# Flamingo-style block on one core: where the attention denominators are inverted and spread, and where the dispatch buffer is zeroed

## The chip, the core and the metric

One core of one Trainium2 chip. Its engines are TensorE (PE; PEld is its weight load), VectorE (DVE), ScalarE (ACT), GpSimd (POOL) and SyncE (SP), which here only issues DMAs; GpSimd issues DMAs too. The metric is device time in microseconds, and lower is better. Each engine works through its own list in order, and waits are semaphore waits, so what stands behind a waiting instruction on its engine waits too.

## The reference

```python
x = x + tanh(g_xattn[0]) * L0_xattn(layernorm(x), ctx)      # 16 heads of 16, softmax over 512 keys
x = x + tanh(g_ffn[0])   * L0_ffn(layernorm(x))             # mixture of 8 experts, top 2, capacity 1280
x = x + tanh(g_xattn[1]) * L1_xattn(layernorm(x), ctx)      # the same attention, other weights
x = x + tanh(g_ffn[1])   * L1_ffn(layernorm(x))             # fp8-quantised linear layer

p = softmax(q k^T / 4);  out = p v;  merged @ wo
buf = zeros(E*C + 1, D).at[pos].set(xk)                     # the dispatch buffer, E*C = 10240 rows of 1 KB
```

x is (8, 512, 256) in float32: 8 batches of 512 tokens, 256 wide. The softmax of both attentions is what the change touches: its exponentials are multiplied with the values first, and the division by their sum comes after.

## The kernel before

The kernel is ten stages, each a block in which all engines start together and which ends when all are done: setup, project, attention (layer 0), route, place, experts, combine, attention (layer 1), merge, quantise.

**Attention** walks through 32 groups (8 batches of 4 groups, each of 4 heads). Per group TensorE forms scores twice. First come eight units for the maxima (`max_unit`, L795), which VectorE reduces (`reduce`, L884) and turns (`turn_maxima`); SyncE then moves the negated maxima nT into four spare rows of q with four DMAs (`subtract_maxima`, L714, tile a_nT). Then come eight score units (`score_unit`, L805), from whose product the maximum is already subtracted; the first unit of a group waits for those four DMAs. ScalarE exponentiates (L867), and TensorE multiplies with v (`values`, L819), whose 17th column of ones gives the sum of the exponentials, the denominator. ScalarE takes the result to osb (L859). SyncE stores it to memory (`outs`, L718) and loads it back as 64 rows of BIG (L722) and as denominators (d_den, L723). GpSimd meanwhile issues the loads of the group four ahead (`load_group`, ten DMAs, L683 to L695), and once a batch the load of v (L765).

**Division** (`class Division`) inverts a batch's denominators on VectorE (`invert`, L612), stores them to `dens` (`store`, L617, four DMAs), loads them back so that each head's row of 1024 reciprocals stands in its 16 partitions (`broadcast`, L626, two DMAs with a source repeated 16 times, into wide), and multiplies BIG by wide on GpSimd (`scale`, L632). Batches 0 to 5 pass through this inside the attention block, 8 to 10 groups late; batches 6 and 7 (`EARLY = 6`) at the start of the next block. SyncE's program in the attention block sets the order:

```python
for n in range(NG):
    if n + 1 < NG:
        subtract_maxima(n + 1)
    if n:
        store_outputs(n - 1)
    if n >= 2:
        load_outputs(n - 2)
    if n >= 2 * G and n % G == 0:
        division.store(e, n // G - 2)
    if n >= 2 * G and n % G == 1:
        division.broadcast(e, n // G - 2)
    if l == 0 and n % G == 2:
        ...                       # one eighth of S.disp <- zeros, L746, 1280 KB
```

The dispatch buffer is zeroed by those eight DMAs and one for `ybuf` (L732), from a zero tile that GpSimd fills (L772), within layer 0's attention.

**Route** (after layer 0) is a pipeline over 8 batches: TensorE's output product of BIG with wo0 (`output`, L935), VectorE's update of X and statistics (L1012, L312, L316), GpSimd's inverse root (`power`, L321, L324), VectorE's normalising (`apply`, L332), TensorE's transposes (`turn`, L917), ScalarE's copy to hT (L988) and TensorE's logits (L924). **Merge** (after layer 1) has the same head with wo1 (L935, L1723, L312 to L332) and takes the largest magnitude (L1732); GpSimd adds a bias (L1688) and first reduces the largest weight over all partitions (`partition_all_reduce`, L1675), for VectorE's chain of ten small steps on the fp8 weights, which stands ahead of its first update. TensorE's output product of batch b waits for `scaled`, for b of 6 and 7 alone.

Of the kernel before, what the change touches and what calls it, by code (L numbers as in the profile page):

```python
# [5 lines left out]
F32 = mybir.dt.float32  # L6
BF16 = mybir.dt.bfloat16
F32R = mybir.dt.float32r
# [6 lines left out]
P = 128  # L15
# [72 lines left out]
def build(nc, a, out, stop=99):  # L88
    ctx = ExitStack()
    with ctx:  # L90
# [49 lines left out]
        S.dens = [dram(f"dens{l}", (B, 2, HG, KD, SEQ)) for l in range(2)]  # L140
# [457 lines left out]
class Division:  # L598


    EARLY = B - 2

    def __init__(self, S, l):
        self.S, self.l, self.ctx = S, l, ExitStack()
        sb = lambda name, shape: self.ctx.enter_context(S.nc.sbuf_tensor(f"d{l}_{name}", shape, F32))
        self.den, self.rec = sb("den", [P, B * G, DH]), sb("rec", [P, B * G, DH])
        self.wide = [sb(f"wide{j}", [P, KD, SEQ]) for j in range(2)]
        self.inverted, self.scaled = S.sem(f"d{l}_inverted"), S.sem(f"d{l}_scaled")
        self.put, self.spread = ([S.sem(f"d{l}_{x}{j}") for j in range(2)] for x in ("put", "spread"))

    def invert(self, e, b):
        e.reciprocal(self.rec[:, b * G:(b + 1) * G, :], self.den[:, b * G:(b + 1) * G, :]).then_inc(self.inverted, 1)  # L612

    def store(self, e, b):
        e.wait_ge(self.inverted, b + 1)
        for g in range(G):
            e.dma_start(self.S.dens[self.l][b, g % 2, :, g // 2, :].rearrange("h (x c) -> h x c", c=DH),  # L617
                        self.rec[:, b * G + g, :]).then_inc(self.put[b % 2], 16)

    def broadcast(self, e, b):  # L620
        e.wait_ge(self.put[b % 2], 16 * G * (b // 2 + 1))
        if b >= 2:
            e.wait_ge(self.scaled, b - 1)
        for x in range(2):
            rows = self.S.dens[self.l][b, x].rearrange("h (o k) t -> h o (k t)", o=1)
            e.dma_start(self.wide[b % 2][x * HALF:(x + 1) * HALF, :, :].rearrange("p k t -> p (k t)"),  # L626
                        rows.broadcast_to([HG, DH, KD * SEQ])).then_inc(self.spread[b % 2], 16)

    def scale(self, e, b):
        e.wait_ge(self.spread[b % 2], 32 * (b // 2 + 1))  # L630
# [4 lines left out]
def attention(S, l):  # L635
# [10 lines left out]
    with ctx:  # L646
# [12 lines left out]
        if l == 0:  # L659
            zeros, zeroed, cleared = sb("zeros", [P, ZROWS, D]), sem("zeroed"), sem("cleared", keep=True)  # L660
            biased, added = sem("biased"), sem("added")
# [1248 lines left out]
```

## Time and profile before

| | us |
|---|---|
| median of 3 runs (2052.09 to 2054.78) | 2053.38 |
| the profiled execution: its time | 2055.22 |
| its span | 2053.5 |
| busy: PE, DVE, ACT, POOL | 1534.2, 1272.3, 906.4, 671.8 |
| attention, layer 0: POOL's first instruction to route's first | 255.3 to 661.1 |
| route: first to the place stage's first instruction | 661.1 to 733.9 |
| attention, layer 1: POOL's first instruction to merge's first | 1508.3 to 1923.9 |
| merge: first to the quantise stage's first instruction | 1923.9 to 1988.2 |

The profiled execution is 1.84 us above the median. The stages follow one another with all engines meeting at each border, so the time is the sum of the stages, and a change in one is worth what that stage becomes shorter or longer.

### The profile page before, as it was taken

How to read it: one execution, taken by the hardware profiler on the slowest of the kernel's cores; microseconds unless marked ns; L12 is line 12 of the kernel's file. 1: busy time of each engine (PE TensorE's matmuls, PEld its weight loads, DVE VectorE, ACT ScalarE, POOL GpSimd, SP SyncE). 2: the span in 40 equal slices, each digit the busy share in tenths (PEclk: the TensorE clock that was granted, in tenths of full speed). 3: DMA queues.
4: the chain of work that ended last, by engine and by line, in shares of the span. 5: the costliest groups of instructions: out<-in, count | busy, mean ns of one | idle time of the engine just before them, and what ended most of it. 6: DMA issues, size and time to landing. Idle time of an engine off the chain costs nothing. (4 is left out here: it accounts for less than half of the span.)

```text
span 2053.5 us, 30167 instructions
## 1 busy us (share of the span) xinstructions
PE 1534.2 (75%) x11799; PEld 1016.4 (49%) x11799; DVE 1272.3 (62%) x1946; ACT 906.4 (44%) x1201; POOL 671.8 (33%) x911
## 2 busy tenths in 40 slices
PE   3867369999998830399999999924539988888634
PEld 2756223333333720399999999922213333333322
DVE  3434179888884650255555555438849977888377
ACT  1433127767776101144444444411107866666304
POOL 0211025555551227300000000048404544443156
PEclk9988669989999955599999999966659999999865
DMA  6655566766663032122122221123355555554102
GB/s 214 194 178 183 162 101 167 178 155 156 157 151 97 21 104 106 62 80 94 45 90 86 86 81 52 37 60 117 121 118 109 140 120 117 132 126 99 61 0 82
DMA packets 150541, 227.78 MB, mean 111 GB/s; under 512 B 45680, under 2 KB 93872, under 8 KB 149248
## 3 DMA queue, kind: packets, MB, share of 16 engines
q1 hardware_dynamic: 116160, 136.68, 23.4%
q0 software_dynamic: 34240, 89.18, 17.7%
q8 instruction: 93, 1.52, 0.3%
q14 instruction: 48, 0.39, 0.1%
HBM read 131.00 MB, written 93.73 MB: 109 GB/s over the span
## 5 line engine op out<-in xcount | busy, mean ns | idle before, releaser
L884 DVE TENSOR_REDUCE a_nmax<-a_ring 128x2 f32<-128x1024 f32 x512 | 608.6, 1218 | 106.1 <-PE a_ring L795 105.8
L867 ACT ACTIVATE a_pexp<-a_ring 128x1024 f32<-128x1024 f32 x512 | 522.5, 1026 | 280.2 <-PE a_ring L805 280.1
L819 PE MATMUL a_pout<-a_pexp,a_v 128*17 128x256 f32 x4096 | 329.9, 396 | 0.7 <-ACT a_pexp L867 0.7
L805 PE MATMUL a_ring<-a_q,a_k 64*128 64x512 f32 x1024 | 266.1, 516 | 61.3 <-DMA a_q<-a_nT 57.9
L795 PE MATMUL a_ring<-a_k,a_q 64*128 64x512 f32 x1024 | 248.0, 482 | 82.2 <-DMA a_q<-qs 72.1
L1402 ACT ACTIVATE e_full<-e_pH,b1T 128x256 f32<-128x256 f32 x320 | 133.6, 468 | 259.3 <-PE e_pH L1362 259.2
L805 PEld LDWEIGHTS a_ring<-a_q,a_k 64*128 64x128 f32 x1024 | 99.3, 190 | 291.8 <-issue 156.1
L1431 DVE TENSOR_TENSOR e_hid_lo<-e_full,e_hid_hi 128x512 fp32r<-128x512 f32 x160 | 110.6, 691 | 157.2 <-ACT e_hid_hi L1410 157.2
L1381 PE MATMUL e_pY<-fc_w_hi,e_hid_hi 128*128 128x256 f32 x640 | 184.3, 288 | 0.2 <-DVE e_hid_lo L1431 0.2
L1362 PE MATMUL e_pH<-e_rowsT_hi,fc_w1T_hi 128*128 128x256 f32 x640 | 182.5, 285 | 1.5 <-DVE e_rowsT_lo L1268 1.5
L1362 PE MATMUL e_pH<-e_rowsT_lo,fc_w1T_hi 128*128 128x256 f32 x640 | 182.3, 285 | 0.0
L1362 PE MATMUL e_pH<-e_rowsT_hi,fc_w1T_lo 128*128 128x256 f32 x640 | 182.1, 285 | 0.0
L1381 PE MATMUL e_pY<-fc_w_lo,e_hid_hi 128*128 128x256 f32 x640 | 181.0, 283 | 0.0
L1381 PE MATMUL e_pY<-fc_w_hi,e_hid_lo 128*128 128x256 f32 x640 | 181.0, 283 | 0.0
L795 PEld LDWEIGHTS a_ring<-a_k,a_q 64*128 64x128 f32 x1024 | 103.7, 199 | 155.5 <-DMA a_q<-qs 73.4
L683 POOL DMA_DIRECT2D a_k<-key_centre x56 | 31.8, 568 | 371.0 <-PE a_ring L805 371.0
L819 PEld LDWEIGHTS a_pout<-a_pexp,a_v 128*17 128x17 f32 x4096 | 68.8, 96 | 139.8 <-issue 136.9
L1362 PEld LDWEIGHTS e_pH<-e_rowsT_hi,fc_w1T_hi 128*128 128x128 f32 x640 | 124.1, 194 | 1.9 <-DVE e_rowsT_lo L1268 1.9
L1362 PEld LDWEIGHTS e_pH<-e_rowsT_lo,fc_w1T_hi 128*128 128x128 f32 x640 | 124.1, 194 | 0.0
L1362 PEld LDWEIGHTS e_pH<-e_rowsT_hi,fc_w1T_lo 128*128 128x128 f32 x640 | 124.1, 194 | 0.0
L1381 PEld LDWEIGHTS e_pY<-fc_w_lo,e_hid_hi 128*128 128x128 f32 x640 | 122.7, 192 | 0.0
L1381 PEld LDWEIGHTS e_pY<-fc_w_hi,e_hid_hi 128*128 128x128 f32 x640 | 122.4, 191 | 0.4 <-DVE e_hid_lo L1431 0.4
(247 smaller groups left out, 2432.3 us busy)
## 6 DMA issues: line engine op xcount, KB each, us to landing
outs<-a_osb SPq DMA_DIRECT2D x64, 256.0 KB, 2.9
fc_raw<-in_L_ffn_fc_w SPq DMA_DIRECT2D x16, 1024.0 KB, 6.8
a_k<-ks POOLq DMA_DIRECT2D x112, 128.0 KB, 3.8
a_q<-qs POOLq DMA_DIRECT2D x112, 128.0 KB, 3.9
disp<-a_zeros SPq DMA_DIRECT2D x8, 1280.0 KB, 15.3
vs<-p_va SPq DMA_DIRECT2D x16, 544.0 KB, 10.9
a_v<-vs POOLq DMA_DIRECT2D x16, 544.0 KB, 5.2
ks<-p_parts_k_hi SPq DMA_DIRECT2D x32, 256.0 KB
```

Source lines behind the costliest of these rows:

```text
L683: e.dma_start(k[j][lo:hi, :, :].bitcast(F32), S.key_centre[l][:, at].rearrange("s (o t) -> s o t", o=1).broadcast_to([hi - lo, 2, SEQ])).t ...
L795: mm = e.matmul(max_bank(m)[:, hh, :], q[j][at, p, t * P:(t + 1) * P], k[j][at, p, :], start=True, stop=True)
L805: mm = e.matmul(score_bank(n * U + i)[:, hh, :], k[j][at, p, t * P:(t + 1) * P], q[j][at, p, :], start=True, stop=True)
L819: mm = e.matmul(pout[n % 2][32 * h:32 * h + VW, at], v[b % 2][:, t, g * HG + h, :], pexp[t][:, h, at], start=(t == 0 and half == 0), stop= ...
L867: e.activation(pexp[t][:, 2 * p:2 * p + 2, :], score_bank(n * U + i)[:, :, :], ACT.Exp).then_inc(exped, 1)
L884: e.tensor_reduce(nmax[n % 2][:, :].rearrange("p (x y t) -> p x y t", x=2, y=2)[:, :, p, t], max_bank(m)[:, :, :], AX.X, ALU.max, negate=T ...
L1362: mm = e.matmul(pH[q][:, f % 2, :], w1T[x][pl][:, k, f * P:(f + 1) * P], rowsT[j][pr][:, k, :], start=(k == 0 and n_pass == 0), stop=(k == ...
L1381: mm = e.matmul(pY[:, t, :], hid[pl][:, f, t * P:(t + 1) * P], w2[x][pr][:, f, :], start=(f == 0 and n_pass == 0), stop=(f == KF - 1 and n ...
L1402: ins = e.activation(full[q % 2][:, f % 2, :], pH[q][:, f % 2, :], ACT.Silu, bias=S.b1T[:, ds(n * KF + f, 1)])
L1431: e.tensor_tensor(hid[LO][:, 2 * q:2 * q + 2, :], full[q % 2][:, :, :], hid[HI][:, 2 * q:2 * q + 2, :], ALU.subtract).then_inc(lo, 1)
```

## The change

Nothing of the division is left in the attention blocks but the denominators' load, which now puts each head's 512 of them into one partition: row 16 b + h of den, 128 rows for 8 batches of 16 heads. At the start of route and of merge VectorE inverts all of them with one reciprocal of 128x512. ScalarE and VectorE cut the result into a high and a low part in fp32r. A matrix pick (GpSimd, 128x2048: the identity with every column 16 times) selects 8 heads' rows, and TensorE multiplies it with both parts (`spread_rows`), so that each head's reciprocals stand in 16 partitions of the PSUM tile pD, one bank; ScalarE copies that to wide (`copy`), twice a batch; GpSimd scales as before, now all 8 batches in these stages. Every output product waits for its batch's scaling. The zero tile, its memset and the nine zeroing DMAs move to route, whose SyncE waits for them.

```diff
 class Division:
-    EARLY = B - 2
...
+        self.den, self.rec = sb("den", [P, SEQ]), sb("rec", [P, SEQ])
+        self.parts = [sb(f"parts{j}", [P, SEQ], F32R) for j in range(2)]
+        self.pick = sb("pick", [P, P, DH], F32R)
...
+    def invert(self, e):
+        e.reciprocal(self.rec[:, :], self.den[:, :]).then_inc(self.inverted, 1)
+
+    def make_pick(self, e):
+        e.tensor_copy(self.pick[:, :, :], self.S.ident[:, :].rearrange("p (h o) -> p h o", o=1).broadcast_to([P, P, DH])
+                      ).then_inc(self.picked, 1)
+
+    def cut_high(self, e):
+        e.wait_ge(self.inverted, 1)
+        e.activation(self.parts[HI][:, :], self.rec[:, :], ACT.Copy).then_inc(self.high, 1)
+
+    def cut_low(self, e):
+        e.wait_ge(self.high, 1)
+        e.tensor_tensor(self.parts[LO][:, :], self.rec[:, :], self.parts[HI][:, :], ALU.subtract).then_inc(self.low, 1)
+
+    def spread_rows(self, e, out, b, k):
+        m = b * KD + k
+        if m == 0:
+            e.wait_ge(self.picked, 1)
+            e.wait_ge(self.low, 1)
+        if m:
+            e.wait_ge(self.copied, m)
...
+        e.matmul(out[:, :], pick, self.parts[HI][:, :], start=True, stop=False)
+        e.matmul(out[:, :], pick, self.parts[LO][:, :], start=False, stop=True).then_inc(self.spread, 1)
+
+    def copy(self, e, src, b, k):
+        e.wait_ge(self.spread, b * KD + k + 1)
         if b >= 2:
             e.wait_ge(self.scaled, b - 1)
...
+        e.activation(self.wide[b % 2][:, k, :], src[:, :], ACT.Copy).then_inc(self.copied, 1)
 
     def scale(self, e, b):
-        e.wait_ge(self.spread[b % 2], 32 * (b // 2 + 1))
+        e.wait_ge(self.copied, (b + 1) * KD)
...
 # attention, SyncE
-                    e.dma_start(division.den[:, n, :], S.outs[l][n, :, DH, :].rearrange("h (x c) -> h x c", c=DH)
-                                ).then_inc(oback[n // G % 2], 16)
+                    e.dma_start(division.den[n * HG:(n + 1) * HG, :], S.outs[l][n, :, DH, :]).then_inc(oback[n // G % 2], 16)
...
-                    if n >= 2 * G and n % G == 0:
-                        division.store(e, n // G - 2)
-                    if n >= 2 * G and n % G == 1:
-                        division.broadcast(e, n // G - 2)
-                    if l == 0 and n % G == 2:
...
 # attention, GpSimd
                 load_v(0)
+                division.make_pick(e)
...
 # route, TensorE
+                spread(0)
+                spread(1)
+                spread(2)
                 output(0)
                 output(1)
                 for i in range(B + 2):
+                    if inside(i + 3):
+                        spread(i + 3)
...
 # route, SyncE
+                e.wait_ge(zeroed, 1)
+                e.dma_start(S.ybuf[E * CAP:E * CAP + P, :], zeros[:, 0, :]).then_inc(cleared, 16)
                 for b in range(B):
...
+                    e.dma_start(S.disp[b * ZROWS * P:(b + 1) * ZROWS * P, :].rearrange("(p r) d -> p r d", p=P),
+                                zeros[:, :, :]).then_inc(cleared, 16)
+                e.wait_ge(cleared, 16 * (B + 1))
...
 # merge, TensorE
+                spread(0)
+                spread(1)
                 for b in range(B):
+                    if inside(b + 2):
+                        spread(b + 2)
+                    e.wait_ge(S.division.scaled, b + 1)
...
 # merge, GpSimd
+                S.division.scale(e, 0)
                 e.wait_ge(wvc, 1)
                 e.partition_all_reduce(wmaxg[:, :], wmax[:, :], P, bass.bass_isa.ReduceOp.max).then_inc(wred, 1)
...
+                    if inside(i + 1):
+                        S.division.scale(e, i + 1)
                     if inside(i):
                         nb.power(e, i, j)
```

How it moves instructions is seen at three places. SyncE's queue in an attention block, from a group's maxima on, before:

```order
L714 DMA a_q<-a_nT 4x8x32 x4
L718 DMA outs<-a_osb 128x512
L722 DMA BIG<-outs 64x1x512
L723 DMA d_den<-outs 128x1x16
L626 DMA d_wide<-dens 64x1x1024 x2
L714 DMA a_q<-a_nT 4x8x32 x4
L718 DMA outs<-a_osb 128x512
L722 DMA BIG<-outs 64x1x512
L723 DMA d_den<-outs 128x1x16
L746 DMA disp<-a_zeros 128x2560
L714 DMA a_q<-a_nT 4x8x32 x4
```


and now:

```order
L728 DMA a_q<-a_nT 4x8x32 x4
L732 DMA outs<-a_osb 128x512
L736 DMA BIG<-outs 64x1x512
L737 DMA d_den<-outs 4x512
L728 DMA a_q<-a_nT 4x8x32 x4
```


The broadcast and the zeroing are gone between the maxima's transfers, and the denominators' load has 4 rows of 512 in place of 128 of 16.

TensorE at the start of route (d_pick and d_parts are the selecting matrix and the cut reciprocals), before:

```order
L935 MATMUL r_pY<-wo,BIG 128x256 x24
L917 MATMUL r_pH<-ident,BIG 128x128 x8
L935 MATMUL r_pY<-wo,BIG 128x256 x8
```


and now, from the sixth and last pair ahead of the first output product:

```order
L635 MATMUL r_pD<-d_parts,d_pick 128x512
L636 MATMUL r_pD<-d_parts,d_pick 128x512
L927 MATMUL r_pY<-wo,BIG 128x256 x16
L635 MATMUL r_pD<-d_parts,d_pick 128x512
L636 MATMUL r_pD<-d_parts,d_pick 128x512
L635 MATMUL r_pD<-d_parts,d_pick 128x512
L636 MATMUL r_pD<-d_parts,d_pick 128x512
L927 MATMUL r_pY<-wo,BIG 128x256 x8
L635 MATMUL r_pD<-d_parts,d_pick 128x512
L636 MATMUL r_pD<-d_parts,d_pick 128x512
```


Six pairs stand ahead of the output products of batches 0 and 1, and two pairs ahead of each of the next.

GpSimd in merge (the rows marked ISA without a tile carry no data), before:

```order
L1675 ISA
L1675 ISA m_wmaxg<-m_wmax 128x1
L321 ISA
L321 TENSOR_SCALAR m_var<-m_mv 128x4
L324 TENSOR_TENSOR m_rstd<-m_var,half 128x4
L632 TENSOR_TENSOR BIG<-BIG,d_wide 128x1024
L321 TENSOR_SCALAR m_var<-m_mv 128x4
```


and now:

```order
L647 TENSOR_TENSOR BIG<-BIG,d_wide 128x1024
L1702 ISA
L1702 ISA m_wmaxg<-m_wmax 128x1
L647 ISA
L647 TENSOR_TENSOR BIG<-BIG,d_wide 128x1024
L320 TENSOR_SCALAR m_var<-m_mv 128x4
L323 TENSOR_TENSOR m_rstd<-m_var,half 128x4
L647 TENSOR_TENSOR BIG<-BIG,d_wide 128x1024
L320 TENSOR_SCALAR m_var<-m_mv 128x4
```


One scaling stands ahead of the all-reduce, another between it and the first batch's power.

## Rows read from the trace of the kernel before

**Rows 1.** Timeline of SyncE's queue, layer 1's attention: start us, us, engine, instruction.

```profile
1563.06 2.63 SPq L714 DMA_DIRECT2D a_q<-a_nT  x4
...
1641.55 1.21 SPq L626 DMA_DIRECT2D d_wide<-dens  x2
1647.29 2.71 SPq L714 DMA_DIRECT2D a_q<-a_nT  x4
...
1665.24 2.71 SPq L714 DMA_DIRECT2D a_q<-a_nT  x4
...
1677.68 2.71 SPq L714 DMA_DIRECT2D a_q<-a_nT  x4
...
1895.02 1.06 SPq L626 DMA_DIRECT2D d_wide<-dens  x2
1900.72 2.71 SPq L714 DMA_DIRECT2D a_q<-a_nT  x4
```

**Rows 2.** The same timeline, layer 0's attention.

```profile
313.27 2.65 SPq L714 DMA_DIRECT2D a_q<-a_nT  x4
...
638.15 2.72 SPq L714 DMA_DIRECT2D a_q<-a_nT  x4
```

**Rows 3.** Timeline of TensorE, layer 1; in brackets idle time before, and its releaser.

```profile
1662.00 0.80 PE L805 MATMUL a_ring<-a_q,a_k 64*128 64x512 f32 x2 [6.86 <-DMA a_q<-a_nT]
```

**Rows 4.** Windows: us; busy of PE, PEld, DVE, ACT, POOL; clock; DMA share; GB/s.

```profile
645.00:646.00 1.00, 1.00 (x14) 0.33 (x18) 0.00 (x0) 1.00 (x2) 0.00 (x0) 1.00 1.13 438
...
674.00:677.00 3.00, 2.51 (x16) 2.33 (x17) 2.97 (x7) 1.02 (x1) 2.37 (x2) 1.00 0.26 105
```

**Rows 5.** Durations: timeline, groups of instructions (x count, busy us, mean ns), and timeline again.

```profile
735.72 0.35 DVE L1085 RECIPROCAL l_rsum<-l_lsum 128x32 f32<-128x32 f32 x1
...
L612 DVE RECIPROCAL d_rec<-d_den 128x64 f32<-128x64 f32 x16 | 8.4, 537 | 46.2 <-PEq L704 46.2
...
L491 ACT ACTIVATE p_w_q_hi<-wq 128x512 fp32r<-128x512 f32 x1 | 0.6, 613 | 0.0
...
40.99 0.63 PE L425 MATMUL p_pJ<-p_cTlo,p_w_k_hi 128*128 128x512 f32 x1
...
214.39 0.40 PE L425 MATMUL p_pJ<-p_cTlo,p_w_k_hi 128*128 128x512 f32 x1
```

**Rows 6.** Timeline of the routing stage, one batch.

```profile
702.83 1.02 ACT L988 ACTIVATE r_hT<-r_pH 128x1024 f32<-128x1024 f32 x1 [6.45 <-PE r_pL L924]
...
704.00 1.06 PE L917 MATMUL r_pH<-ident,BIG 128*128 128x128 f32 x8 [1.26 <-ACT r_hT L988]
...
704.90 3.62 PE L935 MATMUL r_pY<-wo,BIG 128*128 128x256 f32 x16
```

**Rows 7.** Timeline of merge and quantise, and the merge's updates as a group.

```profile
1929.71 0.38 POOL L1675 PARTITION_ALL_REDUCE m_wmaxg<-m_wmax  x1 [23.70 <-DVE m_wmax L1697]
...
1941.45 0.25 POOL L321 TENSOR_SCALAR m_var<-m_mv 128x4 f32<-128x4 f32 x1 [11.36 <-issue]
...
1942.83 2.34 POOL L632 TENSOR_TENSOR BIG<-BIG,d_wide 128x1024 f32<-128x1024 f32 x1
...
1961.64 1.35 DVE L332 TENSOR_SCALAR BIG<-X,m_mv,m_rstd 128x256 f32<-128x256 f32 x4
...
1980.86 4.53 DVE L332 TENSOR_SCALAR BIG<-X,m_mv,m_rstd 128x256 f32<-128x256 f32 x4
...
1993.96 0.38 POOL L1776 PARTITION_ALL_REDUCE q_amg<-q_am  x1 [6.16 <-issue]
2001.81 13.34 POOL L1617 TENSOR_SCALAR q_m<-q_m 128x1024 f32<-128x1024 f32 x3 [7.47 <-issue]
...
L1723 DVE SCALAR_TENSOR_TENSOR X<-m_pY,tg,X x8: 1253/1274/1277, 1933.5 to 1975.3; 128x1024 f32<-128x1024 f32 x8
```

**Rows 8.** All instructions on the zeroing buffer: ns min/median/max; its DMAs to landing.

```profile
L772 POOL MEMSET a_zeros<- x1: 2250/2250/2250, 259.7 to 259.7; 128x2560 f32 x1
...
DMA to landing us min/median/max: 6.5/15.2/18.0
```

More of the change, by code:

```diff
@@ L611, in invert @@
[L611 to L621, printed above, removed]
+        self.S, self.ctx = S, ExitStack()
@@ new lines, in __init__ @@
+        sb = lambda name, shape, dt=F32: self.ctx.enter_context(S.nc.sbuf_tensor(f"d{l}_{name}", shape, dt))
+        self.den, self.rec = sb("den", [P, SEQ]), sb("rec", [P, SEQ])
+        self.parts = [sb(f"parts{j}", [P, SEQ], F32R) for j in range(2)]
+        self.pick = sb("pick", [P, P, DH], F32R)
+        self.wide = [sb(f"wide{j}", [P, KD, SEQ]) for j in range(2)]
+        self.inverted, self.high, self.low, self.picked, self.spread, self.copied, self.scaled = (
+            S.sem(f"d{l}_{x}") for x in ("inverted", "high", "low", "picked", "spread", "copied", "scaled"))
@@ new lines, in spread_rows @@
+    def spread_rows(self, e, out, b, k):
[5 more added lines that the diff above has]
+            e.wait_ge(self.copied, m)
+        heads = P // DH
+        row = b * H + k * heads
+        pick = self.pick[:, row:row + heads, :].rearrange("p h o -> p (h o)")
+        e.matmul(out[:, :], pick, self.parts[HI][:, :], start=True, stop=False)
+        e.matmul(out[:, :], pick, self.parts[LO][:, :], start=False, stop=True).then_inc(self.spread, 1)
@@ L782, in _ @@
                         e.tensor_tensor(x, x, over_tiles(S.w["bo_b"]), ALU.add).then_inc(added, 1)
-                    if n >= 2 * G and n % G == 2:
-                        division.scale(e, n // G - 2)
             @block.tensor
@@ L952, in _, with spread @@
             def _(e):
+                def spread(b):
+                    for k in range(KD):
+                        S.division.spread_rows(e, pD, b, k)
                 def output(b):
-                    if b >= S.division.EARLY:
-                        e.wait_ge(S.division.scaled, b + 1)
+                    e.wait_ge(S.division.scaled, b + 1)
                     if b >= 2:
@@ L1644, in _ @@
                 e.dma_start(w[:, :, :], S.a["L1_ffn_weight"].rearrange("(t p) c -> p t c", p=P)).then_inc(ldw, 16)
-                for b in range(S.division.EARLY, B):
-                    S.division.store(e, b)
-                for b in range(S.division.EARLY, B):
-                    S.division.broadcast(e, b)
                 e.wait_ge(ldw, 16)
@@ L1652, in _, with spread @@
             def _(e):
+                def spread(b):
+                    for k in range(KD):
+                        S.division.spread_rows(e, pD, b, k)
+                spread(0)
+                spread(1)
                 for b in range(B):
-                    if b >= S.division.EARLY:
-                        e.wait_ge(S.division.scaled, b + 1)
+                    if inside(b + 2):
+                        spread(b + 2)
+                    e.wait_ge(S.division.scaled, b + 1)
                     if b >= 2:
@@ L1668, in _ @@
             def _(e):
+                S.division.cut_high(e)
+                for b in range(B):
+                    for k in range(KD):
+                        S.division.copy(e, pD, b, k)
                 e.wait_ge(wtr, 1)
@@ L1673, in _ @@
             def _(e):
+                S.division.scale(e, 0)
                 e.wait_ge(wvc, 1)
```

66 lines of the change are left out of this document (24 added, 42 removed).

## The prediction

> **What bounds the kernel now.** I read the page first for its shares: TensorE is busy 75% and VectorE 62% of the span, so no engine bounds the whole, and a step has to be judged in its own stage. Next I read SyncE's queue in the two attention stages, since the change takes instructions out of it. In layer 1 the set of four small transfers that puts a group's maxima into q (L714) starts every 10.53 us: eight periods lie between 1563.06 and 1647.29 [rows 1]. Then something breaks the beat. The broadcast of batch 0's inverted denominators (L626) is issued at 1641.55, the next maxima at 1647.29, and the sets after them only at 1665.24 and 1677.68: two periods take 30.4 us instead of 21.1, so 9.3 us are lost. Between, TensorE stands in front of a score product and is released by the landing of a_nT [rows 3], about 12 us after those four transfers were issued. VectorE and ScalarE stand too, because everything in the loop hangs on the scores.
>
> Is the broadcast the cause? The value load (L765) and the group loads come in every four groups from the start, and the beat holds for the eight periods before the first broadcast. It also holds after the last one, at 1895.02, with the next maxima at 1900.72, where the group loads have ended [rows 1]. So it takes a broadcast and group loads together, which happens five times in a layer. What a broadcast does to the DMA engines is seen where nearly nothing else runs, in the routing stage: the share is 0.26 at 105 GB/s [rows 4], a quarter of the engines busy and the rest idle. A maxima transfer has four partitions outermost, as a broadcast source has four heads, so both would use the same few engines, in one queue, in order. The Trainium skill, page "DMA: Bandwidth & Descriptors", section "Rules for kernel authors", says that an outermost dimension smaller than 16 confines a DMA to that many engines; by that rule the trace agrees, and the stalls go wholly with the broadcasts. I leave them little chance to stay.
>
> **What goes away.** Layer 1: from the fourth set of maxima at 1563.06 to the 32nd at 1900.72 are 28 periods and 337.7 us; 28 x 10.53 is 294.8; lost are 42.8 us [rows 1]. Layer 0: 28 periods from 313.27 to 638.15, 324.9 us, so 30.0 us are lost [rows 2]. The zeroing transfers (L746) are in layer 0 alone, and its loss is the smaller, so they are not what stalls; taking them out gives nothing of its own here. Nor do the removed inversions: with or without one the period is 10.53. The removed scalings on GpSimd lay in its own idle time. In sum -72.8 us. The bound on one side is this, since a stage cannot run faster than its undisturbed beat (a gain from the lighter denominator load, 4 rows of 2 KB for 128 pieces of 64 B, is below 1 us at the stage's end). On the other side I allow -60, if the value load beside a group load still costs a little.
>
> The new copy that makes pick (128x2048, GpSimd) stands before the first group loads of GpSimd. That queue stands idle there until the first group's scores are done; even at 4.5 ns an element, the dearest GpSimd operation in the trace (13.34 us for three of 1024 columns, [rows 7]), it takes 9 us. Costed at nothing.
>
> **What comes: the routing stage.** Output products started at 661.1 at once, since six batches were already scaled. Now nothing is scaled. The inversion of 128x512: 0.35 us for 32 columns and 0.54 for 64 [rows 5] give 6 ns a column, 3.2 us. Cutting off the high part on ScalarE is 0.61 (L491, [rows 5]), the low part on VectorE taken as the same, 0.3 for handing over: 4.7 us. Then TensorE has to spread batches 0, 1 and 2 before output(0), as its order stands: six pairs of matmuls through one PSUM bank, each followed by ScalarE's copy. A matmul of this shape takes 0.63 us at the low clock (1.2 GHz) and 0.40 at the high one (2.4) [rows 5]; two overlap a little, so a pair is 1.20 or about 0.63. After the idle time I take the low clock. With 0.61 for the copy and 0.15 for handing over a round is 1.96, six without the last copy 11.1. So output(0) starts 15.8 us late (12.3 at the high clock). GpSimd's scale(0), zeroing and scale(1) (2.34, 2.25 and 2.34 us, [rows 7, 8]) follow the first two rounds and end at about that time: hidden.
>
> Later, five batches have a spread in the loop. TensorE idled 1.26 us per batch for ScalarE's copy of hT, 1.02 us [rows 6]; the first pair now fills that. The second waits for ScalarE to do hT (1.02) and then the first pair's copy: the transposes start after 2.5 to 3.1 us in place of 1.26, 1.2 to 1.8 a batch. Five make 6 to 9, and in the first two VectorE is the later one and hides some. I take +21 for the stage, bounds +15 and +27. Zeroing 10.5 MB starts at about 675 and has until 754. At 438 GB/s, which one zeroing transfer reached with little beside it [rows 4], it takes 24 us: hidden.
>
> **What comes: the merge stage.** The same start: parts are ready at 1928.7, six rounds to 1939.8, output(0) 3.7 more (3.62 at the high clock, [rows 6]), 1943.5. VectorE's first update was at 1933.5 [rows 7]. But GpSimd has a second trap. Its all-reduce at 1929.71 is followed by 11.36 us in which GpSimd waits for nothing visible; the one in the quantise stage has 6.16 us of the same ahead of it and 7.47 behind [rows 7]. From the merge's start at 1923.9 to its all-reduce are 5.8. I read this as changing its program there and back. Before, that lay in idle time. Now scale(0) precedes the all-reduce and scale(1) follows it. scale(0) ends at about 1935.0; 5.8 us later the all-reduce (0.38), then VectorE's weight chain, 3.4 us from the all-reduce's end to the first update at 1933.5: now 1944.6. After the all-reduce 7.5 us pass (nothing now burdens DMA there, so I take the shorter), scale(1) ends at 1951.0, the copy and pair of batch 3 and output(1) put the second update at 1956.7. Six more follow, at 6.1 us or above since GpSimd has per batch a scaling and an addition of 2.34 and a power of 1.4 (1941.45 to 1942.83, [rows 7]), where the period was VectorE's (eight updates from 1933.5 to 1975.3, the last ones 5.6 apart): at 6.3 the last is at 1994.5 and not 1975.3. I take +20; bounds +13 (high clock, program change overlapped) and +29 (11.4 us, pairs at the low clock, 6.9 a batch).
>
> **Sum**, against the profiled execution's 2055.2 (span 2053.5): -30.0 - 42.8 + 21 + 20 = -31.8, so 2023.4. The median of the runs is 1.8 lower: **2021.5**.
>
> **Rivals.** (1) *Cheaper start*: pairs at the high clock and program change overlapped, +15 and +13: 2008. For it: TensorE is at the high clock to the end of attention. Against: the idle time after it, and pairs with gaps between. (2) *Dearer merge and routing*: +27 and +29 with the whole gain: 2036. For it: the 11.36. (3) *GpSimd locks VectorE out.* Near the merge's end, where two GpSimd additions stand back to back, VectorE's four normalising steps took 4.53 us in place of 1.35 [rows 7]. A scaling now follows each power in both stages. If it made normalising wait for a whole 2.35 us in all 16 batches: +37.6, 2059, slower; it turns the sign from 2.0 us a batch. Against: in the loop a batch's normalising runs beside the next batch's power, before the scaling starts. The Trainium skill, page "SBUF — State Buffer", section "Who interferes with whom", has the rule: a VectorE instruction in a two-port mode and a GpSimd one block each other for a whole instruction, whoever is first. The row agrees with it; how often it bites is a matter of order. (4) *Zeroing outlasts routing*: at its median 15.2 us from issue to landing [rows 8], eight take 122 us, from 675 to 797, 43 beyond the stage's end: 2065, slower; it decides from 13.6 us a transfer. Against: it was 6.5 when little else ran, and now nothing does. (5) *The stalls stay*, the value load being at fault: 2053.4 + 41 = 2094. Against: eight clean periods with that load in them. (6) The change does not remove the stalls' queueing because the new denominator loads, four rows each, take the same engines: a few us at most, inside the range.
>
> **Chances.** Forecast 0.60, (1) 0.13, (2) 0.15, (3) 0.05, (4) 0.03, (5) 0.04. The range, 2007 to 2037, takes in (1) and (2), which are the bounds of the unknown costs; 0.12 for the others and something for both bounds missed lie outside. (3) could also end within 0.2% (4 us, what a measurement here can tell from no change): faster 0.90, same 0.02, slower 0.08.
>
> **What would show it.** SyncE's maxima sets 10.5 us apart throughout both layers, and no wait for a_nT in them after the first group. The reciprocal near 3.2 us; the first output product 12 to 16 us after the routing stage's start. In the merge a gap of 7 us or more on GpSimd between all-reduce and the second scaling, TensorE waiting behind it, updates over 6 us apart. The zeroing done before the last logits. I am wrong if a stall remains every four groups, if SyncE's wait for the zeroing ends the routing stage, or if normalising takes over 3 us in most batches.

## The result, and the profile after

| us | before | after |
|---|---|---|
| median (4 runs each, taken together) | 2052.86 | 2027.81 |
| ratio, with its 95% interval | | 0.9877 (0.9856 to 0.9899) |
| the profiled execution; its span | 2055.22; 2053.5 | 2028.70; 2027.0 |
| setup and project | 255.3 | 251.4 |
| attention 0 | 405.8 | 372.7 |
| route | 72.8 | 98.1 |
| place, experts, combine | 774.4 | 775.0 |
| attention 1 | 415.6 | 373.2 |
| merge | 64.3 | 92.4 |
| quantise | 65.3 | 64.2 |

The change gains 25.1 us at the median. In the profiled executions the two attentions give 33.1 and 42.4 back, route takes 25.3 and merge 28.1.

**Attention.** The line of the page for the score products, which wait for the maxima, before and after: of 61.3 us idle, 57.9 of them for a_nT, 5.4 are left, and the releaser is another.

```profile
L805 PE MATMUL a_ring<-a_q,a_k 64*128 64x512 f32 x1024 | 266.1, 516 | 61.3 <-DMA a_q<-a_nT 57.9
```

```profile
L802 PE MATMUL a_ring<-a_q,a_k 64*128 64x512 f32 x1024 | 258.9, 502 | 5.4 <-DVE a_nmax L881 4.5
```

SyncE's queue in layer 1, the sets of maxima alone, where [rows 1] had the first stall:

```profile
1551.80 2.63 SPq L728 DMA_DIRECT2D a_q<-a_nT  x4
...
1636.36 2.69 SPq L728 DMA_DIRECT2D a_q<-a_nT  x4
1646.88 2.63 SPq L728 DMA_DIRECT2D a_q<-a_nT  x4
1657.41 2.65 SPq L728 DMA_DIRECT2D a_q<-a_nT  x4
...
1847.25 2.67 SPq L728 DMA_DIRECT2D a_q<-a_nT  x4
```

The beat of 10.53 us holds: 28 periods in 295.45 us, none over 10.9, where they took 337.66. In layer 0 they took 294.88, where [rows 2] had 324.88.

**Route.** VectorE's and TensorE's timelines at its start:

```profile
624.12 3.35 DVE L611 RECIPROCAL d_rec<-d_den 128x512 f32<-128x512 f32 x1 [23.05 <-PEq L718]
628.17 0.69 DVE L623 TENSOR_TENSOR d_parts<-d_rec,d_parts 128x512 fp32r<-128x512 f32 x1 [0.70 <-ACT d_parts L619]
645.29 1.28 DVE L1030 SCALAR_TENSOR_TENSOR X<-r_pY,tg,X 128x1024 f32<-128x1024 f32 x1 [16.43 <-PE r_pY L927]
```

```profile
629.01 0.77 PE L635 MATMUL r_pD<-d_parts,d_pick 128*128 128x512 f32 x1 [12.77 <-DVE d_parts L623]
629.57 0.63 PE L636 MATMUL r_pD<-d_parts,d_pick 128*128 128x512 f32 x1
630.89 0.80 PE L635 MATMUL r_pD<-d_parts,d_pick 128*128 128x512 f32 x1 [0.69 <-ACT d_wide L642]
...
639.53 9.17 PE L927 MATMUL r_pY<-wo,BIG 128*128 128x256 f32 x32
...
652.27 3.72 PE L927 MATMUL r_pY<-wo,BIG 128*128 128x256 f32 x16 [1.68 <-POOL BIG L647]
```

The first output product starts 15.4 us after the stage; the first update 21.2 after it, where it was 5.5. The eight updates then take 53.9 us from the first to the last, where they took 43.8. The zeroing runs meanwhile. Here is the core's engine table in windows; its last three columns are TensorE's granted clock, the busy share of the DMA engines and GB/s:

```profile
641.80:645.80 4.00, 4.00 (x16) 3.32 (x15) 0.51 (x1) 0.00 (x0) 0.00 (x0) 0.75 1.03 428
...
657.80:661.80 4.00, 4.00 (x24) 3.63 (x23) 2.60 (x11) 1.62 (x2) 2.46 (x3) 1.00 1.05 438
...
665.80:669.80 4.00, 4.00 (x28) 3.69 (x26) 0.84 (x3) 0.00 (x0) 3.37 (x2) 1.00 0.00 0
```

It has the engines full to about 663, and its last transfer lands at 665.1, 57 us before the stage's end.

**Merge.** GpSimd's timeline; the stage starts at 1870.36:

```profile
1879.06 2.35 POOL L647 TENSOR_TENSOR BIG<-BIG,d_wide 128x1024 f32<-128x1024 f32 x1 [50.98 <-ACT d_wide L642]
1887.37 0.38 POOL L1702 PARTITION_ALL_REDUCE m_wmaxg<-m_wmax  x1 [5.96 <-ACT d_wide L642]
1894.80 2.33 POOL L647 TENSOR_TENSOR BIG<-BIG,d_wide 128x1024 f32<-128x1024 f32 x1 [7.06 <-issue]
```

Both gaps of the all-reduce, 5.96 and 7.06 us, stand now between the first two scalings. The eight updates, on VectorE:

```profile
1891.35 1.28 DVE L1750 SCALAR_TENSOR_TENSOR X<-m_pY,tg,X 128x1024 f32<-128x1024 f32 x1
...
1904.73 1.28 DVE L1750 SCALAR_TENSOR_TENSOR X<-m_pY,tg,X 128x1024 f32<-128x1024 f32 x1 [10.25 <-PE m_pY L927]
...
1910.31 1.27 DVE L1750 SCALAR_TENSOR_TENSOR X<-m_pY,tg,X 128x1024 f32<-128x1024 f32 x1
...
1918.38 1.28 DVE L1750 SCALAR_TENSOR_TENSOR X<-m_pY,tg,X 128x1024 f32<-128x1024 f32 x1 [2.42 <-PE m_pY L927]
...
1924.56 1.28 DVE L1750 SCALAR_TENSOR_TENSOR X<-m_pY,tg,X 128x1024 f32<-128x1024 f32 x1 [0.51 <-PE m_pY L927]
...
1935.37 1.28 DVE L1750 SCALAR_TENSOR_TENSOR X<-m_pY,tg,X 128x1024 f32<-128x1024 f32 x1 [5.15 <-PE m_pY L927]
...
1949.91 1.28 DVE L1750 SCALAR_TENSOR_TENSOR X<-m_pY,tg,X 128x1024 f32<-128x1024 f32 x1 [2.90 <-PE m_pY L927]
```

All eight come at 21.0, 34.4, 40.0, 48.0, 54.2, 65.0, 70.6 and 79.6 us from the stage's start: after the second, six in 45.2 us. Before a late one ScalarE had waited for GpSimd, and TensorE for ScalarE:

```profile
1919.69 0.60 ACT L642 ACTIVATE d_wide<-m_pD 128x512 f32<-128x512 f32 x1 [5.85 <-POOL BIG L647]
...
1927.78 0.60 ACT L642 ACTIVATE d_wide<-m_pD 128x512 f32<-128x512 f32 x1 [6.08 <-POOL BIG L647]
```

```profile
1928.43 0.80 PE L635 MATMUL m_pD<-d_parts,d_pick 128*128 128x512 f32 x1 [3.45 <-ACT d_wide L642]
1929.03 0.63 PE L636 MATMUL m_pD<-d_parts,d_pick 128*128 128x512 f32 x1
1929.45 9.33 PE L927 MATMUL m_pY<-wo,BIG 128*128 128x256 f32 x32
```

### The profile page after: what moved, and what is told of

Same layout as the page of the kernel before. It is cut to its first block and busy times, and to the rows that moved or that the text cites. A ratio compares the mean times of both kernels' runs of the same rounds, so it can differ in the third digit from the quotient of the medians.

```text
span 2027.0 us, 30246 instructions
## 1 busy us (share of the span) xinstructions
PE 1549.9 (76%) x11862; PEld 1033.1 (51%) x11863; DVE 1271.1 (63%) x1934; ACT 927.0 (46%) x1235; POOL 677.9 (33%) x913
## 3 DMA queue, kind: packets, MB, share of 16 engines
q1 hardware_dynamic: 97600, 127.77, 21.2%
## 5 line engine op out<-in xcount | busy, mean ns | idle before, releaser
L816 PE MATMUL a_pout<-a_pexp,a_v 128*17 128x256 f32 x4096 | 321.5, 387 | 0.7 <-ACT a_pexp L864 0.7
L792 PE MATMUL a_ring<-a_k,a_q 64*128 64x512 f32 x1024 | 243.5, 474 | 74.9 <-DMA a_q<-qs 65.1
L802 PE MATMUL a_ring<-a_q,a_k 64*128 64x512 f32 x1024 | 258.9, 502 | 5.4 <-DVE a_nmax L881 4.5
L697 POOL DMA_DIRECT2D a_k<-key_centre x56 | 31.8, 567 | 318.1 <-PE a_ring L802 318.1
```

The lines of the kernel that those rows point to most:

```text
L697: e.dma_start(k[j][lo:hi, :, :].bitcast(F32), S.key_centre[l][:, at].rearrange("s (o t) -> s o t", o=1).broadcast_to([hi - lo, 2, SEQ])).t ...
L792: mm = e.matmul(max_bank(m)[:, hh, :], q[j][at, p, t * P:(t + 1) * P], k[j][at, p, :], start=True, stop=True)
L802: mm = e.matmul(score_bank(n * U + i)[:, hh, :], k[j][at, p, t * P:(t + 1) * P], q[j][at, p, :], start=True, stop=True)
L816: mm = e.matmul(pout[n % 2][32 * h:32 * h + VW, at], v[b % 2][:, t, g * HG + h, :], pexp[t][:, h, at], start=(t == 0 and half == 0), stop= ...
```

## Experiments

Twelve kernels. Each ratio is to executions of the kernel before that were timed beside it. Setup and project, which none of them touches, took between 241.3 and 259.3 us in their profiled executions. That scatter is as large as some effects, so beside each ratio I give two stretches of the trace that it doesn't enter: from the start of attention 0 to the end of route, and from the start of attention 1 to the end of merge. The last column is TensorE's idle time before score products with a_nT as releaser, over the periods of attention 1. These stretches come from one execution each and scatter too: the merge took 92.4 us in the changed kernel and 89.0 in run 6, where its code is the same, and its six later updates 45.2 and 42.7.

| kernel | ratio (95%) | attention 0 + route | attention 1 + merge | a_nT, layer 1 |
|---|---|---|---|---|
| before | 1 | 478.6 | 479.9 | 32.6 |
| after | 0.9877 | 470.9 | 465.6 | none |
| 1 sixteen rows | 0.9795 (0.9769 to 0.9821) | 469.2 | 445.0 | 7.5 |
| 2 zeroing moved | 1.0048 (1.0029 to 1.0067) | 489.6 | 481.2 | |
| 3 broadcast twice | 1.0566 (1.0531 to 1.06) | 544.5 | 533.9 | 80.3 |
| 4 all-reduce first | 0.9883 (0.9854 to 0.9912) | 474.5 | 460.9 | |
| 5 halves apart, 16 rows | 0.9677 (0.9639 to 0.9716) | 452.7 | 437.9 | |
| 6 zeroing back | 0.9893 (0.9854 to 0.9932) | 472.6 | 463.6 | |
| 7 merge buffers | 0.9882 (0.985 to 0.9915) | 471.9 | 458.8 | |
| 8 no all-reduce | 0.9857 (0.9824 to 0.9891) | 471.1 | 459.2 | |
| 9 halves apart, 4 heads | 0.9763 (0.9705 to 0.982) | 463.9 | 452.0 | 5.5 |
| 10 eight pieces, 4 heads | 0.9979 (0.9951 to 1.0006) | 475.5 | 473.3 | 32.4 |
| 11 change mended | 0.9828 (0.9792 to 0.9863) | 466.8 | 454.8 | |
| 12 scale earlier | 0.9827 (0.978 to 0.9873) | 472.0 | 452.9 | |

### What stalled attention: runs 3, 1, 10, 9 and 5

**Run 3**, the dose. Each broadcast L626 is followed by the same one into a tile `spare`.

> The kernel before with every broadcast issued twice, the second time into a spare tile that nobody reads; four engines are thus busy twice as long. Queueing theory: each of the ten stalls grows by about a broadcast's own time on its engines, so the 73 us lost become 130 to 180: 2105 to 2165 us. Rival (the stall comes from something beside the broadcast, such as the value load, or from the waiting of SyncE for the stored denominators): below 2065 us.

Measured: 2173.43 us. The wait for the maxima grew from 32.6 to 80.3 us in layer 1. Of the waits of TensorE, over the periods of that attention, before and doubled:

```profile
PE a_ring L805 <- DMA a_q<-a_nT: 32.6, 5, 8.6
```

```profile
PE a_ring L807 <- DMA a_q<-a_nT: 80.3, 6, 15.8
```

The longest goes from 8.6 to 15.8 us, and the period behind a broadcast from 15.4 to 16.0 (layer 0) and 16.6 to 19.7 (layer 1) to 26 or 27. The stall is the broadcast's: over the 28 periods the loss against 10.53 us grows from 30.0 to 84.8 us in layer 0 and from 42.8 to 87.1 in layer 1, so in layer 0 by more than the doubling. The time is 8 us above the range that I gave.

**Run 1**, the form, in the kernel before.

```diff
-            rows = self.S.dens[self.l][b, x].rearrange("h (o k) t -> h o (k t)", o=1)
-            e.dma_start(self.wide[b % 2][x * HALF:(x + 1) * HALF, :, :].rearrange("p k t -> p (k t)"),
-                        rows.broadcast_to([HG, DH, KD * SEQ])).then_inc(self.spread[b % 2], 16)
+            for h in range(HG):
+                row = self.S.dens[self.l][b, x, h].rearrange("(o k) t -> o (k t)", o=1)
+                at = x * HALF + h * DH
+                e.dma_start(self.wide[b % 2][at:at + DH, :, :].rearrange("p k t -> p (k t)"),
+                            row.broadcast_to([DH, KD * SEQ])).then_inc(self.spread[b % 2], 16)
```

> The kernel before, with the denominators still going through memory, but each broadcast cut into four transfers of one head (16 destination rows, outermost dimension 16) instead of one with the four heads outermost. Queueing theory (a transfer with 4 outermost rows takes 4 of the 16 DMA engines, and the maxima wait behind it there): the sets of maxima stand 10.5 us apart in both layers, about 73 us go, and nothing is added in the routing and merge stages: 1976 to 1990 us, below both kernels. Rival A (it is the bytes, 0.52 MB a batch beside the group loads, on whichever engines): stalls of 5 to 9 us stay every four groups, 2035 to 2055. Rival B (it is the value load of GpSimd's queue): as before, 2050 to 2056. Rival C (SyncE now issues eight broadcasts in place of two and is itself late with the maxima): the interval after a broadcast is longer by the issue time, 2 to 8 us each, 1985 to 2040.

Measured: 2013.20 us, below both kernels already, and between theory and rival A. The wait for the maxima in layer 1:

```profile
PE a_ring L807 <- DMA a_q<-a_nT: 7.5, 5, 2.3
```

There two of the five stalls are left, one of them here:

```profile
1628.60 4.74 SPq L628 DMA_DIRECT2D d_wide<-dens  x8
1634.36 2.71 SPq L716 DMA_DIRECT2D a_q<-a_nT  x4
...
1649.86 2.71 SPq L716 DMA_DIRECT2D a_q<-a_nT  x4
```

The maxima at 1634.36 follow the broadcast's issue by the usual beat, so SyncE is not late (rival C falls); the next set comes 15.5 us later. From 1625 to 1641 the DMA share is 0.84 to 1.05: broadcast, value load and group loads together fill all sixteen engines. Layer 0 gained less: of its 30.0 us of loss 20.1 are left (layer 1: 11.0 of 42.8), with three periods of 15.2 to 15.4. A zeroing transfer follows each broadcast there; no run tried this form with the zeroing alone taken out.

**Run 10**, the control of run 1: also eight transfers a batch in the same place, but cut by columns, `rows[:, :, c:c + 256].broadcast_to([HG, DH, 256])`, so that four heads stay outermost.

> The kernel before with each batch's broadcast cut into eight transfers, as in the first experiment, but by columns (256 of 1024 each), so that every one still has the four heads outermost. Same number of transfers, same bytes and same place as in the first experiment; only the outermost dimension differs. Four-engine theory: the stalls are as before or larger (the elements are 1 KB and no longer 4): 2050 to 2090 us. Rival (what helped in the first experiment was that eight small transfers let the maxima through): 2005 to 2025 us.

Measured: 2048.34 us, with this wait in layer 1, where before had 32.6 and run 1 7.5:

```profile
PE a_ring L807 <- DMA a_q<-a_nT: 32.4, 6, 7.8
```

The two layers lose 65.7 us over their 28 periods, before 72.8, run 1 31.1. So the number of transfers matters little and the outermost dimension much. The time is 2 us under my range: elements of 1 KB did not lengthen the stalls.

None of the runs changed the maxima's own transfers or their queue. Whether they are held up by the order within SyncE's queue or only by the engines being busy isn't separated.

**Run 5**: run 1, and what piled up is pulled apart; the zeroing is in route, as in the change.

```diff
-                    if n >= 2 * G and n % G == 1:
-                        division.broadcast(e, n // G - 2)
+                    if n >= 2 * G and n % G >= 2:
+                        division.broadcast(e, n // G - 2, (n % G - 2,))
...
-                    if n >= 2 * G and n % G == 2:
-                        division.scale(e, n // G - 2)
+                    if n >= 3 * G and n % G == 0:
+                        division.scale(e, n // G - 3)
+                division.scale(e, B - 3)
```

> The kernel before with the broadcasts of one head each (16 destination rows), now issued in two halves behind the second and third group of a batch's turn instead of all beside the value load, the scaling behind the next batch's first group, and the zeroing in the routing stage as in the change. Theory (the stalls left in the first experiment come where the broadcast, the value load and two group loads fill all 16 engines at once; they are a pile-up and not a price of memory as such): the maxima stand 10.5 us apart in both layers, routing 73 us and merge 60 to 64 us: 1974 to 1986 us. Rival (any broadcast beside group loads costs, the total share of the engines decides): 3 to 6 us stay at most batches, 2000 to 2020 us. Rival 2 (the zeroing, moved, makes the attention of layer 0 slower as it did in the second experiment): layer 0 stays 8 to 12 us above layer 1.

Measured: 1985.54 us, the fastest kernel of the study, 42 us below the changed one. A batch's half broadcast no longer moves the maxima of layer 1, and TensorE never waits for a_nT in its 28 periods:

```profile
1625.85 1.86 SPq L628 DMA_DIRECT2D d_wide<-dens  x4
1631.17 2.71 SPq L715 DMA_DIRECT2D a_q<-a_nT  x4
...
1636.12 1.86 SPq L628 DMA_DIRECT2D d_wide<-dens  x4
1641.70 2.71 SPq L715 DMA_DIRECT2D a_q<-a_nT  x4
```

Layer 0 keeps three periods of 11.1 to 11.8 us. The 28 periods take 297.7 and 295.2 us, in the changed kernel 294.9 and 295.5. Behind the last set of maxima both attentions last 3 us longer than there; batch 5's scaling, which stands there, waits for its broadcast. From the first output product on, route takes 72.0 us and merge 60.0: neither pays anything. Rival 2 falls as well: with hardly a stall there, moving the zeroing costs layer 0 nothing. What of layer 0's gain over run 1 is due to the order and what to the moved zeroing isn't separated; layer 1, which has no zeroing, shows the order alone: 11.0 us of loss in run 1, 0.3 here.

**Run 9**: run 5's order with the old form, one transfer per half with four heads outermost.

> The fifth experiment's order (halves apart, scaling later, zeroing in routing), but each half again as one transfer with the four heads outermost. It separates the two parts of that gain. If the four engines are the cause, each half still keeps them busy for half as long as a whole broadcast: a stall of 1 to 5 us behind most halves, maxima periods of 11.5 to 15, total 2000 to 2035 us. If it was only the pile-up with the value load, the maxima stand 10.5 us apart as in the fifth experiment: 1980 to 1990 us.

Measured: 2004.40 us. Periods of 11 to 12 us and one of 15.4. So order (with the zeroing moved) gives about 48 us, form alone (run 1) 42, and both 66 to 69: they overlap, and neither replaces the other.

### The zeroing: runs 2 and 6

> The kernel before with only the zeroing of the dispatch buffer moved to the routing stage, as in the change; the denominators stay as before. My theory: the zeroing transfers are not what stalls attention, and in routing they are hidden: 2049 to 2057 us, no change. Rival: each zeroing in attention costs a share of the stall; then layer 0 gains 5 to 15 us (2038 to 2048). Other rival: zeroing beside the last two batches' broadcasts holds these back and the routing stage grows by 5 to 15 us (2058 to 2068).

Run 2, the kernel before with the zeroing in route, took 2065.96 us, 11 more. Route grew by less than 1 us (73.6); attention 0 did, by 10.3. Its 28 periods took 335.3 us in place of 324.88: each stall is 1 to 2 us longer. So with the zeroing in attention the stalls behind the broadcasts were shorter. This was no case that I gave, and none of the runs says by what means.

> The changed kernel with the zeroing put back into the attention of layer 0, the denominators as changed. Theory (zeroing is not what stalls, and is hidden in either place): 2023 to 2033 us, maxima 10.5 us apart in layer 0 with at most 2 us lost per zeroing transfer. Rival (zeroing hurts attention by itself): layer 0 is 10 us or more longer, 2036 to 2050. Other rival (the zeroing in routing costs there, through GpSimd's memset and the transfers): 2015 to 2022.

Run 6, the changed kernel with the zeroing back in attention: 2032.44 us, attention 0 and route together 472.6 us in place of 470.9. Where no broadcast stalls, the place makes no difference beyond the scatter (its 28 periods lose 2.0 us).

### The merge: runs 4, 8, 7, 11 and 12

Run 4 is the changed kernel with `scale(e, 0)` behind the all-reduce instead of ahead.

> The changed kernel, with GpSimd's all-reduce of the merge stage moved ahead of the first scaling. My theory (changing GpSimd's program costs about 6 us before the all-reduce and 7 behind, and the change pays both inside the chain of the first two updates): the all-reduce now runs while the reciprocal and the first pairs do, the first update comes 0 to 3 us later than now, the second 2 to 5 us after it instead of 13.4: 8 to 12 us less, 2016 to 2020 us. Rival (the gaps are waits for semaphores or DMA that stay wherever the all-reduce stands; or the six updates that follow are bound by the ring of GpSimd, ScalarE and TensorE so that the earlier start is lost): 2025 to 2031 us.

The first update came at 22.3 us and the second 5.3 later, as expected; the six others took 46.4 and gave part of it back. The stretch is 4.7 us shorter, half of what I expected, and the median, 2031.62 us, doesn't show it: it falls to the rival. The merge, 86.9 us, is only 2.1 below run 6's.

> The changed kernel with the merge stage's all-reduce left out: each partition's own weight maximum is copied in its place, so the weight is scaled row by row and the output differs. Theory (GpSimd's gaps of 5.96 and 7.06 us beside the all-reduce are a change of program, and the first two updates wait for them): the first update comes at 14 to 17 us after the start of the stage in place of 21.0, the second at 21 to 25 in place of 34.4, the merge is 80 to 86 us in place of 92.4: 2014 to 2021. Rival (the gaps are something else, such as the waiting for copies): merge unchanged, 2025 to 2031.

Run 8: GpSimd's gaps of 5.96 and 7.06 us are gone,

```profile
1883.26 2.35 POOL L647 TENSOR_TENSOR BIG<-BIG,d_wide 128x1024 f32<-128x1024 f32 x1 [51.20 <-ACT d_wide L642]
1885.55 0.18 POOL L1702 COPY m_wmaxg<-m_wmax 128x1 f32<-128x1 f32 x1
1887.13 2.43 POOL L647 TENSOR_TENSOR BIG<-BIG,d_wide 128x1024 f32<-128x1024 f32 x1 [1.40 <-ACT d_wide L642]
```

so they belonged to the all-reduce. The second update came at 26.8 us in place of 34.4, but the first at 21.5, no earlier than with it: TensorE's six pairs and a product of 6.00 us, begun at the low clock, last as long. The merge is 85.2 us in place of 92.4, and the six later updates take 45.5. The median, 2025.51 us, missed the range and lies at the edge of the rival's, so the trace decides and not the time. The page "GPSIMD Engine Reference" of the Trainium skill, section "Instruction dispatch", says that the first call of freshly loaded code pays about 6 us that no row shows. The gap ahead, 5.96 us in the changed kernel, agrees in size; the one behind (7.06 there, 7.59 in run 12) comes on top.

> The changed kernel with a third buffer for the spread rows and, in the merge stage alone, two PSUM banks for the pairs in place of one. Theory (after the second update the period is set by a ring: ScalarE's copy waits for GpSimd's scaling two batches back, which stands behind the addition; TensorE's next pair waits for the copy): six updates take 34 to 39 us in place of 45.2, and the first output product comes 3 to 4 us earlier: merge 78 to 84 us in place of 92.4, total 2010 to 2020. Rival (GpSimd's own work of 6.1 us a batch is the period already): the six updates still take 40 us or more and the total is 2020 to 2026. Rival 2 (low clock from TensorE's idle time decides): no change, 2025 to 2031.

Run 7: the six updates took 40.5 us and the merge 84.6. The median is 2029.22 us; the profiled execution took 2012.58, 10 of the difference to the changed kernel's in setup. The six updates are 2.2 to 4.7 us shorter than with one bank and two buffers (run 6 and the changed kernel), so only part of the 45.2 was the buffers'. ScalarE's wait for GpSimd is gone, yet the period of 6.8 us is above GpSimd's own 6.1, so neither theory nor rival is complete. Its waits in that stretch:

```profile
PE m_pY L928 <- POOL BIG L648: 21.3, 5, 10.5
...
DVE X L1752 <- PE m_pY L928: 14.7, 3, 8.6
POOL m_var L320 <- DVE m_mv L315: 14.4, 5, 5.6
```

TensorE waits for GpSimd, VectorE for TensorE and GpSimd for VectorE: none of them is the bound by itself. What both had left out: output(b) waits for scale(b), which GpSimd issues behind the power of batch b - 2, and that needs the update of b - 2. This is a ring over two batches.

Run 11 put runs 4 and 7 together and moved pairs behind output products.

> The changed kernel with its two new costs attacked together: the merge stage's all-reduce ahead of the first scaling, a third buffer for the spread rows, two PSUM banks for the pairs in the merge, and TensorE's pairs of batch 2 (and in the merge of every batch from 2 on) behind an output product instead of ahead of it. Theory: the first update of routing comes 3 to 4 us earlier (17 to 18 us after the start), that of the merge at 15 to 19, the second one at 20 to 25, the six others 5.6 to 6.5 apart: routing 94 to 97 us, merge 74 to 80 us in place of 92.4, total 2008 to 2016. Rival (the low clock after each idle time of TensorE sets the period): the six updates take 40 us or more, merge 82 us or more, total above 2016. In either case it stays above the fifth experiment's 1985.5.

Measured: 2018.41 us. In route the first update came at 16.4 us in place of 21.2, and the stage took 91.7 in place of 98.1. In merge the first update came at 21.2 us and not at 15 to 19: the 7.03 us behind the all-reduce now stand ahead of scale(0), as in run 4. The second came at 25.6, but the six others took 42.4, as the rival has it: merge 80.9. The early start was eaten in the loop, as in run 4.

Run 12 tests the ring by itself. From run 7 it differs in one thing:

```diff
+                S.division.scale(e, 1)
...
-                    if inside(i + 1):
-                        S.division.scale(e, i + 1)
+                    if inside(i + 2):
+                        S.division.scale(e, i + 2)
```

> The seventh experiment's kernel (third buffer, two banks) with GpSimd's scaling in the merge one batch further ahead: scale(i+2) at the head of turn i in place of scale(i+1). Theory (after the second update the period is a ring over two batches: update and statistics 3.3 us, power 1.4, addition 2.35, scaling 2.35, output product 3.6 at the high clock or 5.3 at the low one, together 13.0 to 14.7 for two, 6.5 to 7.4 a batch): with the scaling one batch ahead the same ring spans three batches, 4.3 to 4.9 a batch, so what is left is VectorE's 5.6 or GpSimd's 6.1: the six updates after the second take 34 to 38 us in place of 40.6, and in place of 45.2 in the changed kernel. Rival (the low clock or GpSimd's own work sets it): 40 us or more, as in the seventh experiment. The second update still comes about 31 us after the start, since the all-reduce stays where it was.

Measured: the six updates took 34.7 us, 5.8 apart, where run 7 had 40.5, and the merge 79.3. Its second update and its last:

```profile
1897.81 1.28 DVE L1753 SCALAR_TENSOR_TENSOR X<-m_pY,tg,X 128x1024 f32<-128x1024 f32 x1 [9.14 <-PE m_pY L928]
...
1932.54 1.27 DVE L1753 SCALAR_TENSOR_TENSOR X<-m_pY,tg,X 128x1024 f32<-128x1024 f32 x1
```

TensorE's first products in the loop are short, and of the later three one takes 5.41 us:

```profile
1898.54 3.62 PE L928 MATMUL m_pY<-wo,BIG 128*128 128x256 f32 x16
...
1902.91 3.62 PE L928 MATMUL m_pY<-wo,BIG 128*128 128x256 f32 x16
```

In the changed kernel three of the five rows of one product each from 1898 on are above 5:

```profile
1898.89 5.80 PE L927 MATMUL m_pY<-wo,BIG 128*128 128x256 f32 x16
...
1913.05 5.30 PE L927 MATMUL m_pY<-wo,BIG 128*128 128x256 f32 x16
...
1944.70 5.17 PE L927 MATMUL m_pY<-wo,BIG 128*128 128x256 f32 x16 [5.91 <-POOL BIG L647]
```

Only the order of the scalings was changed against run 7, and the six updates took 5.8 us less, where the same code differed by 2.5 between two executions: the ring is shown. The clock is a part of it: over the six updates the granted clock was 0.81 in the changed kernel, 0.92 in run 7 and 0.95 in run 12. TensorE's busy time over them fell by 1.7 us from run 7 to run 12 (28.8 to 27.1), so shorter products alone don't make the 5.8. The median is 2019.17 us (the profiled execution 2011.50); its interval overlaps with those of run 7 and of the change, so this rests on the stage's times.

## Why the prediction was right

It said 2021.5 us in 2007 to 2037, and 2027.81 was measured. Against its sum of -31.8 the profiled execution changed by -26.5. The mechanism of the gain was right; the merge's loop was not, and scatter elsewhere covered most of that.

- **The stalls, right.** -30.0 and -42.8 were predicted; the periods give -30.0 and -42.2. Runs 3, 1 and 10 show the mechanism: broadcasts with four heads outermost, and little of it due to their number. What the text did not see is that some stalls stay when all sixteen engines are loaded instead (run 1). One reading was not in its row: the set at 1900.72 is the layer's last, so no period behind it can show that the beat holds. That TensorE waits for a_nT five times in layer 1 of the kernel before, and not after 1880, bears the same conclusion.
- **The zeroing "gives nothing of its own here", right for the change and wrong as argued.** I took layer 0's smaller loss as a sign that the zeroing doesn't matter to the stalls. Run 2 shows that without it they are 10 us longer; taking the broadcasts out removes them either way.
- **Route, +21 predicted, +25.3 measured.** The start came as worked out: reciprocal 3.35 us for 3.2, first output product at 15.4 for 15.8. The first product then began at the low clock, and in the loop the updates took 10.1 us longer where I had 6 to 9 and some of it hidden.
- **Merge, +20 predicted, +28.1 measured: the mis-sized term.** The first update came at 21.0 us (20.7 predicted), though run 8 shows that TensorE's chain alone would give the same; the second at 34.4 (32.8). The 5.8 us ahead of the all-reduce were read from a row that can't show them, since before the weight's maximum was itself ready only 5.3 us into the stage; 5.96 came out all the same. The step that failed is "six more follow, at 6.1 us or above ... at 6.3": it added up GpSimd's work per batch. They took 45.2 us, 7.5 apart (42.7 with the same code in run 6). Run 12 shows what was in place of it: a ring of update and statistics, power, addition, scaling and output product, closed over two batches. Its parts are 3.3, 1.4, 2.35, 2.35 and 3.6 (or 5.3 where the clock had fallen), 6.5 to 7.4 a batch. The single bank and the two buffers added the rest (run 7).
- **Elsewhere, luck.** Setup (-3.9), the first groups of attention 0 (-3.1) and quantise (-1.1) gave 8 us that the sum didn't have. That is scatter: the stretch from the attention's start to its fourth set of maxima took 54.8 us in the changed kernel, 57.9 before and 57.9 in run 4, so the memset that is gone from it doesn't explain the 3.1. Without the 8 us the change is worth some 12 us less than predicted, which is what route and merge cost more; the median would then be near 2036, at the range's upper end (an estimate from these differences).
- **Rivals.** VectorE's normalising took 1.35 to 1.77 us in all but one batch of the merge (4.53, as before) and up to 1.53 in route, so rival 3 fell; the zeroing was done 57 us early, so rival 4 did. Its sum was no bound either: it took eight times the time from issue to landing, but the transfers overlapped, and all eight were done 27.3 us after the first was issued, although single ones took up to 20.2; and the turning point of 13.6 us is 13.9 by its own numbers. Further, no stall remained, so 5 did. The new denominator loads stalled nothing (6).

## What to carry to other kernels

When a small transfer on the critical path is late, look at what stands ahead of it in the queues and how many engines that uses, before taking the work off the DMA: here one loop over heads and another place in the order (with the zeroing moved as well) gave about 67 us, and the changed kernel, which paid for the same relief with 53 us of new work at two stage starts, gave 25. When work is put into a pipelined loop, adding up each engine's time per batch gives a lower bound only; follow one batch's result until it releases the same engine again, and divide that by the number of batches that it spans. A price that hid in idle time, like GpSimd's all-reduce, must be counted anew as soon as other work is put on either side of it.

## What the runs showed of the hardware beyond that

- With a transfer of 1.3 MB every four groups the stalls behind the broadcasts with four heads outermost were shorter, by 10 us in a layer (run 2 against the kernel before). By what means stays open.
- With the broadcasts' elements cut from 4 KB to 1 KB the stalls were no longer than before (run 10: 65.7 us lost in both layers, before 72.8).
- TensorE lost clock after some waits: an output product took 3.62 us where the granted clock was 1.00 (2.4 GHz). After waits for a scaling of 2.28 (run 12), 4.06 and 4.08 us (run 11) it took 5.41, 6.34 and 5.32; after waits of 0.59 to 1.79 (runs 7, 11 and 12) it took 3.72. The changed kernel's product of 5.80 us ran its first 4 us at 0.50 (1.2 GHz) and its last 2 at 0.90. Run 12, which only moved a scaling, had 0.95 over its six updates for 0.92 in run 7.
- GpSimd's all-reduce had 5.58 to 6.29 us ahead of it that no row shows when other GpSimd work stood there, and 6.99 to 7.59 behind it (changed kernel, runs 4, 11 and 12; 11.36 in the merge of the kernel before); with a copy in its place both were gone (run 8).
